# One run of 5 KB per partition in place of five of 1 KB: how the ids of the one-hot lookups are laid out in DRAM

## What is computed

```
e = stack([tbl_f[ids[:, f]] for f in range(26)], axis=1)           # 2048 x 26 x 128
all_vecs = concatenate([dense[:, None, :], e], axis=1)              # 2048 x 27 x 128
inter = einsum('bnd,bmd->bnm', all_vecs, all_vecs)
z = concatenate([dense, inter[:, rows, cols]], axis=1)              # the pairs n < m
h = concatenate([z, dense], axis=1)
h = maximum(h @ W_top1 + b_top1, 0); h = maximum(h @ W_top2 + b_top2, 0)
y = h @ W_top3
```

## Time and profile before

| what | us |
|---|---|
| median of three runs | 395.49 |
| span of the profiled execution | 483.2 |
| TensorE matmuls busy in it | 382.4 |
| VectorE busy | 230.3 |
| GpSimd busy | 254.9 |
| ScalarE busy | 144.2 |
| mean granted TensorE clock, share of full speed | 0.898 |

### The profile page before, as it was taken

The page is one execution under the profiler, slowest core; times in us unless marked ns, Lnnn a source line. Parts: engine busy times, 40 slices in busy tenths (PEclk is TensorE's granted clock), DMA queues, the critical chain, the costliest instruction groups (busy, mean ns, idle before and its releaser), DMA issues.

```text
span 483.2 us, 14444 instructions
## 1 busy us (share of the span) xinstructions
PE 382.4 (79%) x6144; PEld 353.0 (73%) x6144; DVE 230.3 (48%) x702; ACT 144.2 (30%) x256; POOL 254.9 (53%) x260
## 2 busy tenths in 40 slices
PE   0756439686788988798799888888988899897977
PEld 0746329676777988587698887788877798786866
DVE  4779428446433375334565456446554545431110
ACT  1156013131322235024141425133324225142422
POOL 6067744655664556556666555655555766553000
PEclk9979859788898879899989988998899979897899
DMA  6998912323141422517242332313131311100000
GB/s 118 230 242 147 264 48 44 85 53 87 48 95 40 51 78 48 82 38 77 75 68 68 51 86 53 82 46 95 43 92 43 97 45 49 38 27 27 4 3 0
DMA packets 25766, 35.86 MB, mean 74 GB/s; under 512 B 6605, under 2 KB 19789, under 8 KB 25743
## 3 DMA queue, kind: packets, MB, share of 16 engines
q1 hardware_dynamic: 16399, 18.72, 20.4%
q0 software_dynamic: 8192, 16.79, 12.0%
q10 hardware_dynamic: 1152, 0.01, 0.1%
HBM read 35.49 MB, written 0.01 MB: 73 GB/s over the span
## 4 chain that ended last, share of the span: by engine, by line
PE 75%; issue 16%; DMA 5%; SPq 2%; POOL 1%; ACT 0%; DVE 0%; POOLq 0%
PE gram L424 12%; PE hid L395 11%; PE look_ps L351 7%; PE vec_act L312 7%; PE look_ps L353 7%; PE look_odd L351 6%; PE look_odd L353 6%; PE hid L402 5%; PE hid L351 4%; PE hid L353 4%; DMA raw<-tbl 3%; PE small L414 2%; DMA vecs<-tbl,ids_sb 2%; POOL vecs L295 1%; PE small L364 1%
## 5 line engine op out<-in xcount | busy, mean ns | idle before, releaser
L295 POOL DMA_INDIRECT vecs<-tbl,ids_sb x256 | 254.7, 995 | 184.5 <-issue 101.0
L572 DVE TENSOR_SCALAR onehot<-step_ids,row_no 125x256 fp32r<-125x256 int32 x640 | 187.9, 364 | 180.1 <-remote 84.4
L424 PE MATMUL gram<-vecs_T 128*27 128x26 f32 x4096 | 61.8, 201 | 52.1 <-issue 51.9
L424 PEld LDWEIGHTS gram<-vecs_T 128*27 128x27 f32 x4096 | 51.5, 113 | 64.7 <-issue 60.6
L547 ACT COPY vecs_T<-vec_act 128x512 f32<-128x512 f32 x64 | 46.1, 728 | 148.1 <-PE vec_act L312 79.3
L351 PE MATMUL look_ps<-onehot,look_hi 125*128 125x256 f32 x256 | 74.0, 319 | 6.7 <-DVE look_lo L580 4.6
L351 PE MATMUL look_odd<-onehot,look_hi 125*128 125x256 f32 x256 | 69.2, 306 | 4.3 <-DVE look_lo L580 2.7
L353 PE MATMUL look_ps<-onehot,look_lo 125*128 125x256 f32 x256 | 69.3, 301 | 2.7 <-issue 2.7
L353 PE MATMUL look_odd<-onehot,look_lo 125*128 125x256 f32 x256 | 64.4, 287 | 0.0
L351 PEld LDWEIGHTS look_ps<-onehot,look_hi 125*128 125x128 f32 x256 | 53.5, 209 | 9.0 <-DVE look_lo L580 4.8
L351 PE MATMUL hid<-onehot,look_hi 125*128 125x256 f32 x128 | 42.6, 355 | 21.0 <-DMA ident<-identity 15.6
(11 more groups left out here) (74 smaller groups left out, 293.3 us busy)
## 6 DMA issues: line engine op xcount, KB each, us to landing
step_ids<-look_ids SPq DMA_DIRECT2D x15, 640.0 KB
raw<-tbl SPq DMA_DIRECT2D x10, 448.0 KB
vecs<-tbl,ids_sb POOLq DMA_INDIRECT x256
vecs<-dense SPq DMA_DIRECT2D x16, 64.0 KB
raw<-tbl SPq DMA_DIRECT2D x10, 52.0 KB
step_ids<-look_ids SPq DMA_DIRECT2D x1, 512.0 KB
w_sb<-w SPq DMA_DIRECT2D x1, 512.0 KB
raw<-w_dense SPq DMA_DIRECT2D x1, 512.0 KB
```

The costliest lines, as they stand in the source:

```text
L295: nc.gpsimd.indirect_dma_start(out=vecs[j][:, 1 + k, :], out_offset=None, in_=tables[k], in_offset=bass.IndirectOffsetOnAxis(ap=ids_sb[:, ...
L424: last = nc.tensor.matmul(gram[s * QUAD:s * QUAD + VECS, g, 0:2 * FOLD], v[:, 0:VECS], v.rearrange("d (h n) -> d h n", h=2)[:, :, 0:FOLD], ...
L572: last = nc.vector.tensor_scalar(onehot[:, i % SLOTS, c, :], step_ids[a][0:LOOK_K, f - a * LOOKUPS // 2, :], row_no[0:LOOK_K, ch:ch + 1], ...
```

## The change

`look_ids` is stored in another order: for each half of the tables and each pair of tiles, the five tables' ids lie next to one another, 5 x 256 numbers in a row. The load of a step then reads one run of 5 KB per partition (4 KB and 1 KB for the two parts of step 0) in place of five runs of 1 KB (four and one). The reordering is done on the host; the bytes loaded, their destination, the number of DMAs, their order and their waits are the same. On TensorE, VectorE, ScalarE and GpSimd every instruction stands where it stood. On SyncE's queue the 16 loads of more than one table keep their places too and change their shape: 128 x 5 x 256 becomes 128 x 1280, and 128 x 4 x 256 becomes 128 x 1024.

```
-                    first, count = a * LOOKUPS // 2 + tables.start, tables.stop - tables.start
-                    src = look_ids[first:first + count, bass.ds(pair * PAIR, PAIR)]
-                    sp.dma_start(step_ids[a][:, tables, :], src.unsqueeze(0).broadcast_to([P, count, PAIR])
-                                 ).then_inc(loaded or step_ids_in[a], 16)
+                    count = (tables.stop - tables.start) * PAIR
+                    src = look_ids[a, bass.ds(pair * STEP_IDS * PAIR + tables.start * PAIR, count)]
+                    sp.dma_start(step_ids[a][:, tables, :].rearrange("p f b -> p (f b)"),
+                                 src.unsqueeze(0).broadcast_to([P, count])).then_inc(loaded or step_ids_in[a], 16)
...
-        "look_ids": np.ascontiguousarray(ids[:, small].T),
+        "look_ids": np.ascontiguousarray(ids[:, small].T.reshape(2, LOOKUPS // 2, -1, 2 * P).transpose(0, 2, 1, 3)
+                                         .reshape(2, -1)),
```

## The result

The changed kernel takes **378.95 us** (median of four runs, 378.38 to 380.38), the kernel before 396.67 in the same comparison (395.31 to 399.94). The ratio is 0.9593, its 95% interval 0.9549 to 0.9638.

The account below looks back on a forecast made before the run. Matmuls on TensorE were taken to bound most of the span, with the start bound by DMA, then VectorE. Faster ids loads start tile 0 between 4.8 and 8.0 us earlier; 7 taken: 395.5 - 7 = 388.5 us, range 384.5 to 395.8.

Parts of the forecast that it names:

- The loads' pace: Step loads of ids: go from 76 to 87 GB/s to 270, because the limit counts runs.
- Rest of step 0: Second part of the first ids load, at the start: 3.4 us less, so tables 1 and 2 are split 3.4 us earlier.
- Step 1: Step 1's ids, between tables 2 and 3 in the start: 3.3 us less; split of table 3 at 21.0.
- VectorE's unbroken stretch: VectorE's work without waits on the start's last six tables: ends 6.7 us earlier, at 44.4.
- The gathers and tile 0: End of the start: gathers go out 4.8 us earlier, tile 0 could start 8.0 us earlier; 7 us taken as gain.
- The loop: Step loads in the loop: their lead is 26 us against 7.5 us needed, so faster loads are worth nothing.
- the pace counts bytes: Rival on the ids loads: they take as long as now, 395.5 us (394.8 by the small-descriptor rule); chance 0.18.
- one place read by all is slower: Rival on the ids loads: all partitions reading the same 5 KB run at 49 GB/s, 10.2 us more, 405.7; chance 0.04.
- the gathers hold tile 0: Rival at the start's end: ids come at 270 GB/s but gathers land late; gain only 4.8 us, 390.7; chance 0.13.
- a bound of the range: Lower end, 384.5 us: the 8.0 us of the start and 3 more for waits on gathers in the loop.

Follow-up runs that it names:

- near_1k: The changed kernel's DRAM layout, but five runs of 1 KB per partition, as the tables stand 64 bytes apart in SBUF: 379.71 us, ratio 0.9614 to the kernel before.
- pitch_9k: The kernel before with rows of `look_ids` padded so that a step's five runs lie 9 KB apart in place of 8: 379.68 us, ratio 0.9613.
- control: The kernel before once more, without an edit, for a second profile: 397.26 us, ratio 1.0055; profile span 393.5 us.
- loop_only: The kernel before, with only the loop's twelve loads reading one run per partition and steps 0 to 3 five runs: 383.37 us, ratio 0.9727.
- start_only: The kernel before, with only the four loads ahead of the loop reading one run per partition: 393.07 us, ratio 0.9945.
- gates_2_far: The kernel before, with gathers of tiles 0 and 1 let out after 2, 4 and 6 finished units in place of 5, 10 and 15: 389.52 us, ratio 0.9854.
- pitch_16k: The kernel before with rows of `look_ids` padded so that a step's five runs lie 16 KB apart: 394.87 us, ratio 1.0022.

## Why the prediction was too small

**The loads' pace: right in size, wrong in cause.** 270 GB/s was taken, 296 to 308 came. That is luck: the reason given, "the limit counts runs", is refuted by near_1k (five runs, 352 GB/s) and pitch_9k (330). What tells fast from slow is whether the five places that all 128 partitions read lie 8 or 16 KB apart, and the change happened to end that too. For the same reason the rule on small descriptors that the rival drew on (the Trainium skill, "DMA: Bandwidth & Descriptors", section "Why small descriptors are slow (HBM only)") had nothing to decide here: its 7% would be, as an estimate, some 0.2 us of a load of 2.4. The same page has in "Latency and other measured facts" a rule that is nearer: where the rows that the partitions copy lie a large power of two apart, bandwidth is lost (164 GB/s at 2 MiB, 103 at 4 MiB), and a few KiB of padding give it back. The runs agree that padding is a cure (1 KB of it), but at a pitch of 8 KB, between the runs of one partition, which the rule doesn't name.

**Rest of step 0: right.** Table 1 was to be split at 12.6, and is at 12.98; control had 15.88, so 2.9 us for the 3.4 of the sum.

**Step 1: right.** The split of table 3 was forecast at 21.0 and stands at 20.63; control had 28.09.

**VectorE's unbroken stretch: right.** Forecast to end near 44.4; the last split ends at 44.48, in control at 51.52, 7.0 us later. (It isn't quite unbroken: VectorE stands 0.75 us before 42.21, behind TensorE's wait for gathers.)

**The gathers and tile 0: right at tile 0, partly by luck, and too large at the end.** The first group behind a gate starts at 22.31 (forecast 20.9), the first gathers of tile 1 at 32.65 (31.7; control 36.51). That is a gain of 3.9 us, less than tile 0's 7.1, so GpSimd's lead shrank; the wait of 3.65 us at 38.54 is new. Tile 0 starts at 46.79 for the forecast 47. The 7 us had been chosen between 4.8 and 8.0, and the 8.0 counted a wait of 1.38 us as won that control doesn't have; what came are VectorE's 7.0. And the step to the end was wrong: the sum took tile 0's 7 us off the whole time, but the first round waits for the gathers, which gained 3.9. Beside fast loop loads the start's new loads save 3.7 us (383.37 for loop_only, 379.71 for near_1k), alone 3.1, which control's half per cent leaves in doubt.

**The loop: this step failed.** It said: "A faster load is worth nothing there, and would be covered up to three times its present length." For VectorE, the load's reader, that holds, and only its wait was looked at. The load's other effect was left out: while it crawls, the gathers issued behind it on another engine's queue don't move. The runs put the term, which had zero, at 12.8 us (the kernel before, 396.14, against loop_only) to 13.4 (start_only, 393.07, against near_1k, 379.71, where the loop's loads are fast too); the 8.9 us net of the rounds (5.0 + 5.9 - 2.0) are less because part of the start's 7.1 is lost in them. Up to 96 us GpSimd is only just ahead of TensorE, so gathers held for 7 to 8 us end in waits, and those in half the clock. The second round's loss is another: the gaps at line 424, 5.4 us, of which more below. From 156.50 on control's rounds lose nothing with the same slow loads. In the recorded profile the slow TensorE covered all of this; the prediction saw that it might ("waits on gathers in the loop, which a TensorE with 77 us of issue time hides"), allowed 3 us for it in the range, and didn't work it out from GpSimd's lead. Yet for the start it had reckoned with a gather that lands late behind a load of ids (the 7.87 us), and the recorded profile shows the same in the loop. From 79.50 to 84.50, where by the prediction only a step's ids move, GpSimd sent out five gathers, and its queue has no line:

```profile
q1 hardware_dynamic: 424, 0.43, 45.8%
...
vecs<-tbl,ids_sb POOLq DMA_INDIRECT x5
```

That a gather waits for the load is shown: 19 of 224 packets moved in 7 us against 192 between loads, and with a longer lead of GpSimd's (gates_2_far) the waits for gathers are gone though the loads are as slow as before. The Trainium skill ("DMA: Bandwidth & Descriptors", section "Queues, rings and completion order") says that a DMA engine takes turns between its queues, a packet from each. By that the gathers would have had their share of the half-idle engines; in this stretch the trace doesn't agree. Why the gathers don't move is open.

**The gaps at line 424** go with slow loads in the loop (from 57 to 350 us they come to 5.4 us in control, 10.9 in start_only, 11.9 in gates_2_far and 4.3 in pitch_16k, and to at most 1.1 in each kernel with fast loads there). That they are fetches of instructions held up like the gathers is argued only. In control, one packet of the instruction queue lands between 117.0 and 117.5, just when the load is through, and TensorE's gap of 2.77 us ends at 119.87; another lands between 143.0 and 143.5, and the gap ends at 145.46 (the two in between, behind 121.0 and 130.5, fall in no load). From 150 to 230 that queue moves nothing, and there are no gaps. No experiment took a fetch away.

**The rivals.** That the pace counts bytes is refuted (83 GB/s became 308). That one place read by all is slower is refuted for the 5 KB of a step; for the 1 KB of one table it holds (82 GB/s, and 172 with a copy for each). That the gathers hold tile 0 came true only as a wait inside step 1. The one on the record that came nearest to the cause was no rival but a bound of the range.

**Left open.** Which addresses share a place: 8 and 16 KB do for broadcast runs, 8.5 KB does by half, 9 KB doesn't; why 128 copies at multiples of 8 KB don't wasn't tried further. It is not known either why ids of the old layout went at 326 GB/s for 0.6 us in the start, nor why the rounds after the second take 2.0 us more in the changed kernel (TensorE is busy there 0.7 us longer in the third round, 42.24 for 41.57, and 1.1 us in all).

## What to carry to other kernels

A transfer that nobody waits for can still set the time: ask what is issued behind it on every other queue while it is in flight, and how much lead those have, before its speed is counted at nothing. Where a DMA reads one source into all partitions in several runs, look at the distance between them first; a pad of the row may do as much as a new layout. And before the slack of a profiled execution is used in a sum, its span should stand beside the time of the runs: 87.7 us between them meant that every wait for gathers in the loop had been covered.

## What the hardware showed that was not expected

- A read of five runs of 1 KB by all 128 partitions took 8.0 us at 107 GB/s with the gathers that shared it (runs 16 KB apart), 4.0 us at 208 (8.5 KB), 2.3 us at 330 (9 KB), 2.2 us at 352 (adjacent), and 2.3 us at 328 from 128 separate copies (runs 8 KB apart in each).
- During a slow load the gathers' queue stood still from 109 to 115 us with DMA engines about half idle; one gather took 10.69 us from issue to landing.
- One table's ids, a single run of 1 KB per partition, came at 82 GB/s when all partitions read the same 1 KB and at 172 when each read its own copy.
